# Reading the self-attention keys and queries back from DRAM with four 48-row loads, and a new order of steps, in a one-core decoder layer

## The reference, cut to what matters

```python
x = layernorm(x + self_attention(x))          # 16 heads of 8; q and k l2-normalised over all 128 channels, divided by a temperature
x = layernorm(x + cross_attention(x, ctx))    # 16 heads of 8; causal, with a relative-position term from Er
x = layernorm(x + experts(x))                 # top-1 of 8 experts, 128 -> 2*512 (gated) -> 128
```

## Time and profile before

| | us |
|---|---|
| median of 3 runs | 351.69 (351.1 to 353.1) |
| the profiled execution, its time | 353.29 |
| the profiled execution, its span (first to last instruction) | 351.5 |
| PE busy | 247.2 |
| DVE busy | 208.9 |
| ACT busy | 125.9 |
| share of the span on the chain that ended last: PE, DVE, DMA | 45%, 19%, 18% |

### The profile page before, as it was taken

One profiled execution on the slowest core, in us unless ns is written; L12 is line 12 of the kernel. 1 busy time (PEld: TensorE's weight loads), 2 busy tenths in 40 slices (PEclk: granted clock), 3 DMA queues, 4 the chain that ended last, 5 costly groups with the idle time before them and its releaser, 6 DMA issues.

```text
span 351.5 us, 8165 instructions
## 1 busy us (share of the span) xinstructions
PE 247.2 (70%) x3284; PEld 177.2 (50%) x3285; DVE 208.9 (59%) x579; ACT 125.9 (36%) x286; POOL 69.2 (20%) x105
## 2 busy tenths in 40 slices
...
PEclk9999999665698599799879899995597658999995
...
GB/s 81 154 123 29 13 203 148 120 267 212 25 151 134 103 206 156 27 76 171 70 91 136 10 90 17 129 275 138 77 4 32 2 1 75 67 300 118 249 66 1
DMA packets 28413, 38.18 MB, mean 109 GB/s; under 512 B 4447, under 2 KB 22093, under 8 KB 27608
## 3 DMA queue, kind: packets, MB, share of 16 engines
...
## 4 chain that ended last, share of the span: by engine, by line
PE 45%; DVE 19%; DMA 18%; issue 6%; ACT 4%; SPq 3%; POOL 3%; POOLq 0%; ACTq 0%; DVEq 0%
DMA QS<-parts_a 6%; DMA w_sb<-parts_a 6%; DVE negm L881 5%; PE SB L1196 5%; PE MB L1227 5%; PE SA L1106 4%; PE SB L1192 4%; PE MB L1069 4%; PE MA L1069 3%; SPq L403 3%; PE SA L1305 3%; PE SB L1305 3%; DMA parts_a<-SpA 3%; PE MA L1081 2%; PE SB L1313 2%
## 5 line engine op out<-in xcount | busy, mean ns | idle before, releaser
L881 DVE TENSOR_REDUCE negm<-SA 128x2 bf16<-128x512 f32 x64 | 41.6, 691 | 28.0 <-PE SA L1106 26.5
L688 ACT ACTIVATE P<-SA 128x512 f32<-128x512 f32 x64 | 35.5, 602 | 4.9 <-PE SA L1121 3.3
L1106 PE MATMUL SA<-KS,QS 96*128 96x256 bf16 x64 | 16.1, 358 | 22.8 <-DMA QS<-parts_a 20.9
L941 DVE TENSOR_REDUCE negm<-MB 128x4 bf16<-128x512 bf16 x32 | 22.0, 687 | 12.9 <-PE MB L1069 12.5
L1106 PE MATMUL SA<-w_sb 96*128 96x256 bf16 x64 | 16.3, 361 | 15.4 <-DMA w_sb<-parts_a 11.1
L646 ACT ACTIVATE Sb<-SB 128x512 bf16<-128x512 f32 x24 | 14.3, 597 | 33.1 <-PE SB L1196 30.4
L936 DVE TENSOR_TENSOR Sm<-SB,Sb 128x512 bf16<-128x512 f32 x16 | 11.0, 690 | 21.2 <-ACT Sb L646 20.3
L1106 PEld LDWEIGHTS SA<-KS,QS 96*128 96x128 bf16 x64 | 4.9, 109 | 33.2 <-DMA QS<-parts_a 22.5
L602 POOL TENSOR_TENSOR rs<-ve,half 128x2 f32<-128x2 f32 x8 | 5.7, 716 | 74.9 <-DVE ve L845 74.9
L719 ACT ACTIVATE P2b<-SB 128x1024 f32<-128x1024 f32 x16 | 16.3, 1025 | 7.8 <-PE SB L1215 7.3
L1106 PEld LDWEIGHTS SA<-w_sb 96*128 96x128 bf16 x64 | 5.0, 112 | 24.9 <-DVE negm L881 11.8
...
## 6 DMA issues: line engine op xcount, KB each, us to landing
...
```

What stands on the lines that cost most here:

```text
L688: a.activation(P1[:, grp % 2, kt, 2 * i:2 * i + 2, :].rearrange("p h t -> p (h t)"), SA[:, bank_a("st", b, u), :], ACT.Exp).then_inc(s["ex ...
L881: v.tensor_reduce(out=negm1[:, qt, :, hp], in_=SA[:, bank_a("d", b, u), :].rearrange("p (g k) -> p g k", g=2), axis=AX.X, op=ALU.max, nega ...
L941: v.tensor_reduce(out=negm2[:, qb, :], in_=MBb[:, 0:512].rearrange("p (c k) -> p c k", c=4), axis=AX.X, op=ALU.max, negate=True).then_inc( ...
L1106: last = mm(SA[:, bank, i * NT:(i + 1) * NT], QSs[b % 2][0:2 * SR, i * (H // 2) + hp, qt * P:(qt + 1) * P], KSs[b % 2][0:2 * SR, hp, :], s ...
```

## The change

The keys are read back in two halves of 48 rows, each with the access pattern that the query halves have already, between the query halves. There are four loads instead of three, so the counts on `qs_in` go from 48 to 64 a batch. The bytes stay the same. The loads of cross-attention are left as they were. `ORDER` is new: it holds the same steps in another sequence.

```diff
-PACED_BY = {("A1", "qsin"): ("qs_in", 48, 48), ("A1", "d"): ("sa_full", 16, 1), ("A1", "shT"): ("m_in", 16, 16), ("A2", "st"): ("st_full", 16, 1),
+PACED_BY = {("A1", "qsin"): ("qs_in", 64, 64), ("A1", "d"): ("sa_full", 16, 1), ("A1", "shT"): ("m_in", 16, 16), ("A2", "st"): ("st_full", 16, 1),
...
             def q_k_out(b):
-                wait(sp, "qs_in", b * 48)
+                wait(sp, "qs_in", b * 64)
...
                 wait(sp, "pa_out", b * 96 + 96)
-                load(KSs[b % 2][0:2 * SR, :, :], parts_a[1].rearrange("w (d g j) t -> g (w d) (j t)", g=2, j=H // 2), "qs_in")
                 for g in range(2):
                     rows = slice(g * SR, (g + 1) * SR)
                     load(QSs[b % 2][rows, g * (H // 2):(g + 1) * (H // 2), :], half_stack(parts_a, 0, g), "qs_in")
+                    load(KSs[b % 2][rows, :, :], half_stack(parts_a, 1, g), "qs_in")
...
                 if u == 0:
-                    pe.wait_ge(s["qs_in"], b * 48 + 48)
+                    wait(pe, "qs_in", b * 64 + 64)
```

The moves in `ORDER`, first for batches 0 and 1:

```diff
-    A1.qkv.0 A1.qkn.0 A1.qkT.0 A1.qsin.0 A1.k5.0 A1.vcp.0 A1.qkv.1 A1.k4.0 A1.k2.0 A1.d0.0 A1.d1.0 A1.d2.0
-    A1.d3.0 A1.d4.0 A1.d5.0 A1.d6.0 A1.d7.0 A1.d8.0 A1.d9.0 A1.d10.0 A2.xpb.0 A1.d11.0 A1.d12.0 A1.d13.0
-    A1.d14.0 A2.cx.0 W.v6.0 A1.d15.0 A1.qkn.1 A1.shT.0 A1.qkT.1 W.bl0.0 A1.qsin.1 A2.k2T.0 W.bl1.0 W.u0.0 B.v.0
...
-    A2.pv2.0 A2.pv3.0 A1.d0.1 A1.d1.1 A2.nm1.0 A1.d2.1 W.bl2.0 A1.d3.1 A2.oT.0 A1.d4.1 A2.proj.0 A2.ln1.0
-    A1.k0.1 A2.x1T.0 A2.q2T.0 A1.d5.1 A1.d6.1 A1.d7.1 A1.d8.1 A1.d9.1 A1.d10.1 A1.d11.1 A1.d12.1 A1.d13.1
-    A1.d14.1 A1.d15.1 A1.shT.1 A1.vcp.1 B.build.0 B.rest.0 A1.qkv.2 B.sc0.0 B.sc1.0 B.tr0.0 A2.st0.1 A1.qkn.2
...
+    A1.qkv.0 A1.qkn.0 A1.vcp.0 A1.qkT.0 A1.k5.0 A1.qkv.1 A1.qsin.0 A1.k2.0 A1.d0.0 A1.d1.0 A1.d2.0 A1.d3.0
+    A1.d4.0 A1.d5.0 A1.d6.0 A1.d7.0 A1.d8.0 A1.d9.0 A1.d10.0 A1.d11.0 A1.d12.0 A1.d13.0 A1.d14.0 A2.cx.0
+    A1.d15.0 A2.xpb.0 A1.k4.0 A1.qkn.1 A1.shT.0 A1.qkT.1 A1.k6.0 W.bl0.0 A2.st0.0 A2.st1.0 A1.qsin.1 A2.k2T.0
+    A2.st2.0 A2.st3.0 A2.st4.0 A2.st5.0 A2.st6.0 A2.st7.0 A2.pv0.0 A2.pv1.0 A2.st8.0 A2.st9.0 A2.nm0.0 A2.st10.0
+    A2.st11.0 W.bl1.0 A2.st12.0 A2.st13.0 A2.st14.0 W.v6.0 A1.k3.1 A2.st15.0 A1.k1.1 A2.pv2.0 A1.d0.1 A2.pv3.0
+    A1.d1.1 A2.nm1.0 A1.vcp.1 A1.d2.1 B.v.0 A2.oT.0 A1.d3.1 A2.proj.0 A2.ln1.0 A1.k0.1 A1.qkv.2 A2.x1T.0
+    A2.q2T.0 A1.d4.1 A1.d5.1 A1.d6.1 A1.d7.1 A1.d8.1 A1.d9.1 A1.d10.1 A1.d11.1 A1.d12.1 A1.d13.1 A1.d14.1
+    A1.d15.1 A1.shT.1 B.build.0 B.sc0.0 A1.qkn.2 B.rest.0 B.sc1.0 B.tr0.0 A1.qkT.2 A2.st0.1 A2.st1.1 B.sc2.0
+    A2.st2.1 B.tr1.0 A2.cx.1 A2.st3.1 B.sc3.0 W.bl2.0 A2.st4.1 A2.st5.1 A2.xpb.1 A2.pv0.1 B.tr2.0 A2.st6.1
+    A2.st7.1 B.sh0.0 B.sh1.0 B.tr3.0 B.sh2.0 A2.st8.1 A2.pv1.1 W.u0.0 A2.st9.1 B.sc4.0 A2.st10.1 W.bl3.0
...
```

More of the change, by code:

```diff
@@ L71 @@
-    A2.st10.1 B.sh3.0 A2.st11.1 B.sc4.0 A2.k2T.1 A2.st12.1 A2.st13.1 B.sc5.0 A2.st14.1 A2.st15.1 A2.pv2.1
-    A1.d0.2 B.tr4.0 A2.pv3.1 A1.d1.2 A2.nm1.1 A1.d2.2 A1.vcp.2 W.bl3.0 A1.d3.2 A2.oT.1 A1.d4.2 A2.proj.1 W.u2.0
-    B.tr5.0 A1.d5.2 A2.ln1.1 A1.d6.2 A1.qkv.3 B.pv0.0 A1.d7.2 A2.x1T.1 B.sh4.0 B.nm0.0 A2.q2T.1 A1.d8.2 B.sh5.0
-    W.v7.0 A1.d9.2 B.sc6.0 A1.d10.2 B.sc7.0 B.tr6.0 A1.d11.2 A1.d12.2 B.tr7.0 B.sh6.0 A1.d13.2 A1.d14.2 B.sh7.0
-    A1.d15.2 A1.shT.2 B.build.1 B.pv1.0 B.rest.1 B.sc0.1 B.nm1.0 B.sc1.1 B.tr0.1 B.ln2.0 A2.st0.2 A2.st1.2
```

39 lines of the change are left out of this document (20 added, 19 removed).

## The result

The changed kernel takes 321.12 us (median of 4 runs, 319.84 to 330.98), the kernel before 351.39 on the same chip: a ratio of 0.916 (0.910 to 0.922). On another chip it took 319.62 against 348.71, a ratio of 0.919 (0.912 to 0.925). Some executions of any of these kernels, like the one of 330.98, run a few per cent longer at a lower granted clock; the medians contain them, the ratios leave them out. The profiled execution took 320.35 us, its span is 318.6.

The account below looks back on a forecast made before the run. The prediction took each batch's read-back before the scores, its key load on two DMA engines, as the bound. Gains 6.0 + 3.8 + 4.0 + 4.7 + 0 = 18.5 us took 353.3 to 334.8; range 325 to 342.

Parts of the forecast that it names:

- The loads: Read-back before each batch's scores: about 6.2 us instead of 12.5 to 11.8, worth 5.9 us each (3.3 to 7.2).
- Rival C: Read-back before the scores: key halves keep to two DMA engines, the tail stays, 356 to 357 us; chance 3%.
- the charge for the order: Losses set against the faster loads between score steps, such as 1.3 and 0.5 us after d0.0, 2.5 and 1.5 after d0.1.
- From d0.1 to d0.2: First score of batch 1 to that of batch 2: 50.5 us becomes 46.4, gain 4.0.
- the 1.5 us for the stores: Third read-back, before d0.2: landing delayed 1.5 us (0 to 5) by traffic of `bl2`, `u0` and `bl3`.
- From d0.0 to d0.1: First score of batch 0 to that of batch 1: 35.3 us becomes about 31.5, gain 3.8.
- the 1.3 for `bl1`: Second read-back, before d0.1: store `bl1` starts when it is half done and costs 1.3 us (0 to 2.6).
- From d0.2 to d0.3: First score of batch 2 to that of batch 3: 57.9 us becomes about 53, gain 4.7 (2.5 to 6).
- From d0.3 to the end: First score of batch 3 to the end, 176.7 us: no read-back, gain 0 (gain 2 to loss 2).
- A: Whole kernel: order pays fully, stores cost nothing, clock stays higher; loads 23.6 plus order 2 to 3, 326 us; chance 17%.
- B: Batches 1 to 3: stores and Z behind `x1T` eat half, gain 11, 341 us; chance 18%.
- D: Whole kernel: loads give what they should but new waits eat all of it, 350 to 353 us; chance 2%.

Follow-up runs that it names:

- loads_only: The change without the new `ORDER` (four loads, old order), against the kernel before: 327.96 us, ratio 0.938.
- cols_split: Kernel before with four loads in the old order, keys halved by columns, each key load still 96 rows led by 2: 353.99 us, ratio 1.011.
- order_only: The new `ORDER` alone with the one key load of before, against the kernel before: 361.31 us, ratio 1.035.
- warm_before: Kernel before plus 50, 68 and 53 small matmuls in PE's waits for the stacks of batches 1 to 3: 352.94 us, ratio 1.001.

## Why the prediction was wrong, step by step

**The loads: right.** No tail, 5.6 to 6.5 us until a read-back had landed where 6.2 (5.0 to 8.7) was forecast, the first score at 24.5 for 25, and 23.2 us for the four alone where 23.6 was the middle. That the sum fits so well is partly luck: in `loads_only` the three intervals and the first score win 7.0, 3.7, 6.2 and 6.5 us where each was put at 5.9. Rival C is excluded by `loads_only`, whose first score comes 5.5 us after SP's first load; `cols_split` shows what C would have looked like.

**The step that failed** is the charge for the order. Four loads at 5.9 us are 23.6; the forecast of 18.5 thus lets the order and the waits behind the loads take 5.1 us away. Measured, the loads gave 23.2 and the order added 7 to them. The charge failed above all in "From d0.1 to d0.2": "x1T comes 3 to 4 us later ... So `sc0.0` starts some 27 us after d0.1 instead of 24.7: a loss of 2.5", and the 1.5 us for the stores. Measured: x1T 1.0 us later, sc0.0 at d0.1 + 23.1, d0.2 at 18.1 behind it, 41.2 in place of 46.4. 3.9 of the 5.2 us lie before sc0.0 and 1.3 behind it. In the prediction's own sum, 29.7 + 16.7, the first term was 25.3 (qkT.2 at 79.4) and the second 15.9. Three things were mis-sized. `qkv.2` was charged at the 3.9 us that it took in its old place; that is its price at granted clock 0.50, and in the new place it takes 2.46. Z's way was credited 1 us for the stores that left; its load came 3.6 us behind the writes in place of 5.8, 2.2. And I let the read-back lie under traffic of `bl2`, `u0` and `bl3` for 1.5 on top of its 15.2: it landed 15.2 us after qkT.2 and PE's own 16 us, which the prediction has right, set d0.2, so PE had no wait there at all. I had put together for each stretch a loss from one move and a gain from another. At sc0.0 the runs show that two of the moves lift two limits of the same gap, which gives 1.0 us only together; that the same holds for the rest of the 7 us is not shown.

**From d0.0 to d0.1**, 31.5 forecast, 29.6: SP's first load came 24.0 us after d0.0 (48.47 less 24.52), just the 23.5 and 0.5 of the prediction. The rest was put at 7.5, that is 11.8 less 5.6 and 1.3 more, and took 5.6: the 1.3 for `bl1` was not there (`bl1` was issued at 49.91, beside the read-back), and the read-back was 0.6 shorter. For the slow load the charge would have been too small, it was 3.7 us in `order_only`.

**From d0.2 to d0.3**, 53.2 forecast, 51.5 and 48.9: 1.7 to 4.3 too long. The loads alone have 51.4.

**From d0.3 to the end** I forecast nothing and 4.9 us were gained. Most of it isn't the change's: from sc0.3 to the experts' stage the profiled execution of before took 45.9 us, and `cols_split` and `warm_before`, with the same work there, 41.9 and 42.5. Its granted clock is the nearest difference: 0.71 against 0.81 in `warm_before` (rows above). From d0.3 to the end these two need 173.9 and 173.4 us where the profile of before has 176.7. 1.4 us are the order's (173.2 in `loads_only` to 171.8), which I had put at 0 within "gain 2 to loss 2". The forecast counted from this one profile, 353.3, which was 1.9 us above the median of 351.4; from median to median it misses 12.1 us.

**The rivals.** A, "the order pays fully", 326, was the nearest in kind, at 17%; it named the stores and the clock as reasons, and was still 5 us too high. I bounded the order's worth by 2 to 3 us, and it is 7. Of its reasons, that the stores cost nothing on the path held, and the clock did rise, by an amount whose worth wasn't separated. B and D did not occur.

**What stays open:** by which moves the order saves its 7 us. Only 1.0 us was built up again from the old order, at sc0.0, and it didn't reach the kernel's time. Some 2 of the 7 us lie in small moves between sc0.0 and d0.2, and some 2 to 4 in batches 2 and 3, which I can place only by stretches. The spread of one kernel's profiles there, 51.5 and 48.9 for the same stretch, is as large.
